# Holding each four gathers until the last four have landed, in a two-layer graph transformer on one core

## The chip, the cores and the metric

The kernel runs on one core of a Trainium2 chip. The metric is the time of one execution on the device, in microseconds, as a median over runs; lower is better. The engines are TensorE (PE in the rows, its weight loads PEld), VectorE (DVE), ScalarE (ACT), GpSimd (POOL) and SyncE (SP). Each has its own instruction queue, and they meet only through semaphores.

## The reference, cut to what matters

A graph has 3,125 nodes with 256 features and 50,000 edges sorted by destination. Two layers follow each other. Each adds a graph attention, a linear attention over all nodes and a mixture of experts to the node features.

```python
h = (x @ W.T).reshape(n, H, D)                       # layer 0: 8 heads of 32
alpha = einsum(h[src], a_src) + einsum(h[dst], a_dst) + sum(relu(edge_attr @ edge_W.T + b) * h[dst])
attn = segment_softmax(leaky_relu(alpha), dst)
out = segment_sum(h[src] * attn, dst)
...
# layer 1: two such convolutions in a row, 4 heads of 128, then 1 head of 256, without edge features
```

What matters here is `h[src]`: for every edge, the row of its source node is fetched from a table in HBM.

## The kernel before, in words

The edges lie in 196 blocks of 256, and the work goes over 220 windows (a block, cut where the destination tile of 128 nodes changes). The program is a list of stages. Each stage is a block in which all five engines run their own instruction lists; the next stage begins when all have ended.

A gather is one `indirect_dma_start` on GpSimd: 128 rows of a node table in HBM, chosen by an index column, are fetched into SBUF. GpSimd computes the descriptors, then the DMA engines move the rows. The gathers increment a semaphore of the buffer that they fill (`K.gath[q]`), and whoever uses the rows waits for it.

- `linear_attention_l0`: TensorE, ScalarE and VectorE compute the linear attention of layer 0 (25 tiles, five chunks of five). Beside it, GpSimd gathers the table rows (1,088 B) of the first 30 pairs of blocks, 4 gathers for each pair (line 793, three buffers, `GS` = 4). SyncE waits for each pair and stores it to HBM in edge order (lines 779 and 781); the gather of pair g waits for the store of pair g-3.
- `edge_scores_l0`: for 110 groups of two windows, VectorE makes one-hot matrices, TensorE multiplies (lines 1050 and 1054), ScalarE evacuates (1064), VectorE multiplies and sums (1110 and 1115). Beside it, GpSimd gathers the other 68 pairs, 4 gathers each (line 1033, six buffers). ScalarE copies the score terms out of each pair (line 1072, `sources`), in its own order between the evacuations, and SyncE stores the pair (1006). The gather of pair n waits for the copy and the store of pair n-6. ScalarE stands at the copy of pair n until its rows have landed, at a place in its list that is spread evenly over the 110 groups (`due`).
- `gather_rows` (line 1160) sets rows aside for every window of `STAGED` (66 of the 220, for each of the two convolutions of layer 1): 2 gathers for each window, five buffers, and a store to HBM for each window (`store_rows`, line 1170). It is called in five stages: `linear_attention_l1` (16 windows), the scores of the first convolution (40), its softmax (10), the scores of the second convolution (58) and its softmax (8). Rows have 2,064 B in the first convolution and 1,028 B in the second.
- `aggregate` (line 1603) gathers the remaining 154 windows of each convolution directly, 2 gathers a window, and is not touched.

Of the kernel before, what the change touches and what calls it, by code (L numbers as in the profile page):

```python
# [37 lines left out]
SUB = EB // P  # L38
# [674 lines left out]
def linear_attention_l0(prog, K, A):  # L713


    with Stage(prog, "mix0") as st:
        GS, QR = 2 * SUB, 3
# [35 lines left out]
        s_gath, gathered = K.gath, list(K.gathered)  # L753
# [9 lines left out]
        @block.sync  # L763
        def _(sp):
            sp.dma_start(wkv[:, :, 0:D], A["m0_wkt"].rearrange("(k p) n -> p k n", p=P)).then_inc(s_wkv, 16)
            sp.dma_start(wkv[:, :, D:2 * D], A["m0_wvt"].rearrange("(k p) n -> p k n", p=P)).then_inc(s_wkv, 16)
            load_rows(sp, s_w, gain[:, 0, :], A["m0_kg"])
            load_rows(sp, s_w, gain[:, 1, :], A["m0_vg"])
            load_rows(sp, s_w, shift[:, 0, :], A["m0_kb"])
            load_rows(sp, s_w, shift[:, 1, :], A["m0_vb"])  # L770
            sp.dma_start(wot[:, :, :], A["m0_wot"].rearrange("(k p) n -> p k n", p=P)).then_inc(s_w, 16)
            sp.dma_start(wq[:, :, :], A["m0_wq"].rearrange("(k p) n -> p k n", p=P)).then_inc(s_w, 16)
            sp.dma_start(enc_w[:, :], A["g0_enc"]).then_inc(s_encw, 16)
            load_rows(sp, s_bias, bias[:, 0, :], A["g0_b"])
            load_rows(sp, s_bias, bias[:, 1, :], A["m0_bo"])
            for g in range(EARLY0):
                q = g % QR
                sp.wait_ge(s_gath[q], gathered[q] + 16 * GS * (g // QR + 1))
                sp.dma_start(K.edge_h0[g * GS * P:(g + 1) * GS * P, :].rearrange("(k p) r -> p k r", p=P),
                             rows[:, q, :, 0:ROW0]).then_inc(s_kept[q], 16)  # L780
                sp.dma_start(home_of[g], rows[:, q, :, ROW0:ROW0 + H0]).then_inc(s_kept[q], 16)
            for q in range(QR):
                sp.wait_ge(s_kept[q], 32 * len(range(q, EARLY0, QR)))

        @block.gpsimd
        def _(pool):
            st.clear_stale(pool)
            for g in range(EARLY0):
                q = g % QR
                if g >= QR:  # L790
                    pool.wait_ge(s_kept[q], 32 * (g // QR))
                for k in range(GS):
                    pool.indirect_dma_start(rows[:, q, k, :], None, K.table0[:, :],  # L793
                                            bass.IndirectOffsetOnAxis(ap=K.src_blk[:, g * GS + k:g * GS + k + 1], axis=0)).then_inc(s_gath[q], 16)
# [147 lines left out]
def edge_scores_l0(prog, K, A):  # L942
# [6 lines left out]
    with Stage(prog, "score0") as st:  # L949
        G, Q, U2, QR = 2, 5, 2, 6  # L950
        GS = G * SUB
# [15 lines left out]
        s_gath, gathered = K.gath, list(K.gathered)  # L967
# [23 lines left out]
        @block.sync  # L991
        def _(sp):
            def load(g):
                q = g % Q
                if g >= Q:
                    sp.wait_ge(s_hot, g - Q + 1)
                    sp.wait_ge(s_en, G * (g - Q + 1))
                planes = K.edge_rows[g:g + 1, :].rearrange("g (m a e) -> g m a e", m=G, a=2)[:, :, 0, :]
                sp.dma_start(rel[:, q, :].rearrange("p (m e) -> p m e", m=G),
                             planes.partition_broadcast(P).rearrange("p g m e -> p (g m) e")).then_inc(s_load[q], 16)  # L1000
                sp.dma_start(attr[:, q, :], bass.AP(tensor=K.attr_parts.tensor, offset=g * (G * EB), ap=[[0, 3], [W * EB, R // 3], [1, G * EB]])).then_inc(s_load[q], 16)

            def keep(n):
                g, q = EARLY0 + n, n % QR
                sp.wait_ge(s_gath[q], gathered[q] + 16 * GS * (n // QR + 1))
                sp.dma_start(K.edge_h0[g * GS * P:(g + 1) * GS * P, :].rearrange("(k p) r -> p k r", p=P),
                             rows[:, q, :, 0:ROW0]).then_inc(s_kept[q], 16)

            for g in range(Q):
                load(g)  # L1010
            for g in range(groups):
                for n in range(due(g), due(g + 1)):
                    keep(n)
                if g + Q < groups:
                    load(g + Q)
            for n in range(due(groups), late):
                keep(n)
            sp.wait_ge(s_spread, W)
            sp.dma_start(pen, bass.AP(tensor=K.pen.tensor, offset=0, ap=[[L, C], [0, H], [1, L + 1]])).then_inc(s_pen, 16)
            for q in range(QR):  # L1020
                sp.wait_ge(s_kept[q], 16 * len(range(q, late, QR)))
            sp.wait_ge(s_pen, 16)

        @block.gpsimd
        def _(pool):
            st.clear_stale(pool)
            for n in range(late):
                g, q = EARLY0 + n, n % QR
                if n >= QR:
                    pool.wait_ge(s_copied, len(homes) + n - QR + 1)  # L1030
                    pool.wait_ge(s_kept[q], 16 * (n // QR))
                for k in range(GS):
                    pool.indirect_dma_start(rows[:, q, k, :], None, K.table0[:, :],  # L1033
                                            bass.IndirectOffsetOnAxis(ap=K.src_blk[:, g * GS + k:g * GS + k + 1], axis=0)).then_inc(s_gath[q], 16)
# [117 lines left out]
def gather_rows(pool, K, table, rows, windows, s_free):  # L1152

    Q = rows.shape[1]
    for n, w in enumerate(windows):
        q = n % Q
        if n >= Q:
            pool.wait_ge(s_free[q], 16 * (n // Q))
        for s in range(SUB):
            pool.indirect_dma_start(rows[:, q, s, :], None, table,  # L1160
                                    bass.IndirectOffsetOnAxis(ap=K.src_col[:, w * SUB + s:w * SUB + s + 1], axis=0)).then_inc(K.gath[q], 16)
# [19 lines left out]
def edge_scores_l1(prog, K, name, H, C, RW, table, kept, A):  # L1181
# [4 lines left out]
    with Stage(prog, name) as st:  # L1186
# [61 lines left out]
        @block.gpsimd  # L1248
        def _(pool):
            st.clear_stale(pool)  # L1250
            gather_rows(pool, K, table, held, STAGED[first:early], s_free)
# [115 lines left out]
def segment_softmax(prog, K, name, H, C, keep_max=None, RW=0, table=None, kept=None, A=None):  # L1367
# [8 lines left out]
    with Stage(prog, name) as st:  # L1376
# [43 lines left out]
        @block.gpsimd  # L1420
        def _(pool):
            st.clear_stale(pool)
            if blanks:
                pool.memset(zeros[:, :], 0.0).then_inc(s_zeros, 1)
            if late:
                gather_rows(pool, K, table, held, STAGED[early:], s_free)
# [822 lines left out]
def linear_attention_l1(prog, K, A):  # L2249

    KD = LH * LD
    with Stage(prog, "mix1") as st:
# [32 lines left out]
        @block.gpsimd  # L2285
        def _(pool):
            st.clear_stale(pool)
            gather_rows(pool, K, K.table1, held, STAGED[0:FIRST[H1]], s_free)
# [717 lines left out]
```

## Time and profile before

| | us |
|---|---|
| median of three runs | 3081.26 |
| range of the runs | 3078.65 to 3088.63 |
| span of the profiled execution | 3595.1 |

The profiled execution has no other time than its span: from its first instruction to its last 3595.1 us, 513.8 us more than the median of the runs. The rows below are from that one execution, with times in us from its first instruction. Busy means that an engine executes; idle time in brackets stands ahead of an instruction, with what ended it ("issue" and "remote" mean that the profile shows nothing that ended it just then). Ends of TensorE's matmuls are modelled.

### The profile page before, as it was taken

The numbers are of one execution on the slowest core, as the hardware profiler recorded it, in microseconds if no ns is written. First come the engines' busy times: TensorE is split into PE (matmuls) and PEld (weight loads), VectorE is DVE, ScalarE is ACT, GpSimd is POOL, SyncE is SP. The second block draws the span as 40 slices with busy tenths as digits, with TensorE's granted clock in tenths as the row PEclk, the third lists the DMA queues.
The fourth block names the chain that finished last, engine by engine and source line by source line (L and its number), as shares of the span: only waits on it lengthen the run. The fifth ranks groups of instructions, "written<-read, shape, count | busy, mean of one in ns | idle before, by whom it ended". The sixth has DMA issues, their size and how long they took to land. (4 is left out here: it accounts for less than half of the span.)

```text
span 3595.1 us, 47970 instructions
## 1 busy us (share of the span) xinstructions
PE 2251.7 (63%) x11012; PEld 1557.3 (43%) x11013; DVE 2033.2 (57%) x4073; ACT 1091.0 (30%) x3339; POOL 1519.1 (42%) x1534
## 2 busy tenths in 40 slices
PE   3333567677578738976666498897703556666543
PEld 3112233333456535553455377675602434444432
DVE  6328455556788844325268577677504645555733
ACT  3103232333300122215200465664400055556311
POOL 1660544453000020112453777775472166666044
PEclk9755566655799959998867799998855677777577
DMA  4870555565287628862697787786686344444066
GB/s 140 227 203 0 157 176 178 166 184 170 93 237 230 195 86 258 268 221 92 242 392 255 231 249 245 242 245 203 186 220 172 85 126 128 127 130 130 7 203 192
DMA packets 450407, 655.70 MB, mean 182 GB/s; under 512 B 68320, under 2 KB 329310, under 8 KB 449683
## 3 DMA queue, kind: packets, MB, share of 16 engines
q1 hardware_dynamic: 330003, 351.74, 31.7%
q0 software_dynamic: 84944, 255.17, 24.1%
q10 hardware_dynamic: 35296, 46.90, 3.7%
q8 instruction: 66, 1.08, 0.1%
q14 instruction: 98, 0.80, 0.1%
HBM read 485.21 MB, written 169.74 MB: 182 GB/s over the span
## 5 line engine op out<-in xcount | busy, mean ns | idle before, releaser
L1603 POOL DMA_INDIRECT xn<-table,src_col x572 | 617.5, 1080 | 246.1 <-issue 155.7
L1646 PE MATMUL sum_h_ps<-xn,sum_h_hot 128*128 128x261 f32 (+1 forms) x1936 | 556.4, 439 | 226.3 <-DVE xn L1660 103.2
L1646 PEld LDWEIGHTS sum_h_ps<-xn,sum_h_hot 128*128 128x128 f32 x1936 | 404.2, 217 | 369.5 <-issue 169.9
L1160 POOL DMA_INDIRECT arena_a<-table,src_col x264 | 268.0, 1015 | 388.9 <-issue 321.1
L1669 DVE TENSOR_TENSOR arena_a<-arena_a,sum_h_ps 128x522 f32 (+1 forms) x440 | 246.4, 560 | 305.2 <-issue 115.4
L1033 POOL DMA_INDIRECT arena_b<-table,al x272 | 257.5, 947 | 360.1 <-ACT arena_a L1072 185.5
L1054 PE MATMUL score_ps_hd<-arena_a,score_hot 128*128 x1320 | 289.4, 382 | 0.0
L1110 DVE TENSOR_TENSOR xn<-xn,score_ps_hd 128x528 f32<-128x528 f32 x220 | 154.4, 702 | 228.1 <-remote 144.5
L1660 DVE TENSOR_TENSOR xn<-xn,al 128x514 f32<-128x514 f32 (+1 forms) x352 | 242.9, 690 | 45.8 <-issue 19.4
L1754 PE MATMUL sum_ps<-xn,sum_hot 128*128 128x264 f32 x880 | 210.6, 393 | 52.2 <-DVE sum_hot L1764 34.2
L1050 PE MATMUL score_ps_en<-enc_rows,score_attr 30*128 30x256 bf16 x440 | 119.4, 367 | 186.5 <-DVE xn L1110 122.5
L1064 ACT ACTIVATE xn<-score_ps_en 128x512 f32<-128x512 f32 x220 | 129.9, 595 | 343.0 <-PE score_ps_en L1050 204.4
L1754 PEld LDWEIGHTS sum_ps<-xn,sum_hot 128*128 128x128 f32 x880 | 162.4, 190 | 100.4 <-issue 75.5
L1054 PEld LDWEIGHTS score_ps_hd<-arena_a,score_hot 128*128 128x128 bf16 x1320 | 146.7, 125 | 125.2 <-issue 78.0
L1646 PE MATMUL sum_h_ps<-arena_b,sum_h_hot 128*128 128x261 f32 x704 | 177.1, 400 | 31.2 <-DVE arena_b L1660 26.2
L1768 DVE TENSOR_TENSOR xn<-xn,al 128x528 f32<-128x528 f32 x220 | 154.6, 703 | 32.1 <-DMA xn<-edge_h 30.7
L1615 ACT ACTIVATE sum_h_hot<-sum_h_away,sum_h_one 128x256 f32<-128x256 f32 x220 | 111.7, 508 | 191.0 <-DMA score_attr<-attr_parts 78.9
L1631 ACT ACTIVATE xn<-xn,al 128x129 f32<-128x129 f32 x528 | 167.3, 388 | 0.0
L1646 PEld LDWEIGHTS sum_h_ps<-arena_b,sum_h_hot 128*128 128x128 f32 x704 | 137.9, 198 | 61.6 <-DVE arena_b L1660 29.8
L793 POOL DMA_INDIRECT xn<-table,al x120 | 117.0, 975 | 91.2 <-issue 91.2
L1115 DVE TENSOR_REDUCE al<-xn 128x16 f32<-128x528 f32 x220 | 152.9, 695 | 0.0
L1610 ACT ACTIVATE sum_h_away<-iota_row,rel_col 128x128 f32<-128x128 f32 x440 | 149.1, 386 | 0.0
(531 smaller groups left out, 4127.5 us busy)
## 6 DMA issues: line engine op xcount, KB each, us to landing
xn<-edge_h SPq DMA_DIRECT2D x220, 264.0 KB, 3.0
edge_h<-arena_b SPq DMA_DIRECT2D x68, 528.0 KB
arena_b<-kept SPq DMA_DIRECT2D x66, 516.0 KB
xn_t<-edge_rows SPq DMA_DIRECT2D x110, 256.0 KB, 4.7
score_h_hot<-hots SPq DMA_DIRECT2D x220, 128.0 KB
kept<-arena_a ACTq DMA_DIRECT2D x40, 516.0 KB
xn<-kept SPq DMA_DIRECT2D x66, 257.0 KB
arena_a<-in_f_w SPq DMA_DIRECT2D x16, 1024.0 KB, 8.6
```

Of the source, the lines that this page charges most:

```text
L1033: pool.indirect_dma_start(rows[:, q, k, :], None, K.table0[:, :], bass.IndirectOffsetOnAxis(ap=K.src_blk[:, g * GS + k:g * GS + k + 1], ax ...
L1054: ins = pe.matmul(ps_hd[:, m, s, 0:D + H], lhsT=hot[:, q, edges[s]], rhs=near[:, window, c, :], start=(c == 0), stop=(c == 2))
L1110: dve.tensor_tensor(prod[:, w % U3, :].rearrange("p (s d) -> p s d", s=SUB), enc[:, m, :].rearrange("p (s d) -> p s d", s=SUB), ps_hd[:, m ...
L1115: dve.tensor_reduce(al[:, w * SUB:(w + 1) * SUB, :], prod[:, w % U3, :].rearrange("p (s h r) -> p s h r", s=SUB, h=H), AX, ALU.add).then_i ...
L1160: pool.indirect_dma_start(rows[:, q, s, :], None, table, bass.IndirectOffsetOnAxis(ap=K.src_col[:, w * SUB + s:w * SUB + s + 1], axis=0)). ...
L1603: pool.indirect_dma_start(rows[w][:, s, 0:RW], None, table, bass.IndirectOffsetOnAxis(ap=K.src_col[:, w * SUB + s:w * SUB + s + 1], axis=0 ...
L1631: ins = act.activation(cols, cols, ACT.Copy, scale=al[:, w * SUB + 1, h:h + 1])
L1646: ins = pe.matmul(ps[:, u, b, 0:part], lhsT=hot[:, w % QH, s, :], rhs=rows[w][:, s, b * part:(b + 1) * part], start=(s == 0), stop=(s == S ...
L1660: dve.tensor_tensor(view, view, al[:, bass.ds(w * SUB, HALF), :].rearrange("p s h -> p (s h)").unsqueeze(2).broadcast_to([P, HALF * H, RW ...
L1669: dve.tensor_tensor(out, out, ps[:, j % U2, :, 0:part], ALU.add).then_inc(s_acc, 1)
L1754: ins = pe.matmul(ps[:, bass.ds(banks[j % 4], 1), 0:ROW0].rearrange("p a c -> p (a c)"), lhsT=hot[:, q, s, :], rhs=rows[:, q, s, :], start ...
L1768: dve.tensor_tensor(view, view, al[:, bass.ds(w * SUB, SUB), :].unsqueeze(3).broadcast_to([P, SUB, H, R]), ALU.mult).then_inc(s_msg, 1)
```

## The change

In each of the three places where such gathers are issued, GpSimd waits, before it issues the next four, until the semaphore shows that the last four have landed. The waits that were there (for a free buffer) stay. No gather, buffer or store is added or moved.

```diff
                 if g >= QR:
                     pool.wait_ge(s_kept[q], 32 * (g // QR))
+                if g:
+                    pool.wait_ge(s_gath[(g - 1) % QR], gathered[(g - 1) % QR] + 16 * GS * ((g - 1) // QR + 1))
                 for k in range(GS):
...
                     pool.wait_ge(s_kept[q], 16 * (n // QR))
+                if n:
+                    pool.wait_ge(s_gath[(n - 1) % QR], gathered[(n - 1) % QR] + 16 * GS * ((n - 1) // QR + 1))
                 for k in range(GS):
...
         if n >= Q:
             pool.wait_ge(s_free[q], 16 * (n // Q))
+        if n and n % 2 == 0:
+            pool.wait_ge(K.gath[(n - 1) % Q], K.gathered[(n - 1) % Q] + 16 * SUB * ((n - 1) // Q + 1))
         for s in range(SUB):
```

## Rows read from the trace of the kernel before

**Rows 1.** The page's first line.
```profile
span 3595.1 us, 47970 instructions
```
**Rows 2.** Windows: stretch, length, PE, PEld, DVE, ACT, POOL busy (instructions), PEclk, DMA, GB/s.
```profile
104.00:360.00 256.00, 93.59 (x212) 44.43 (x212) 123.88 (x158) 45.77 (x50) 117.03 (x120) 0.62 0.48 137
360.00:927.00 567.00, 384.44 (x1760) 173.38 (x1760) 324.82 (x582) 167.90 (x511) 257.54 (x272) 0.62 0.56 165
984.00:1253.00 269.00, 216.07 (x896) 166.53 (x896) 229.48 (x661) 16.40 (x42) 0.00 (x0) 0.99 0.75 221
...
2010.00:2502.00 492.00, 416.81 (x1760) 341.61 (x1760) 362.37 (x661) 299.24 (x1101) 356.51 (x318) 0.94 0.78 237
...
2579.00:2847.00 268.00, 91.19 (x983) 70.36 (x983) 108.83 (x268) 0.00 (x0) 109.84 (x116) 0.54 0.62 176
...
2875.00:3337.00 462.00, 299.19 (x880) 200.50 (x880) 234.60 (x442) 264.49 (x881) 311.35 (x308) 0.75 0.46 126
```
**Rows 3.** Windows of 10 us in the scores of the second convolution.
```profile
2710.00:2720.00 10.00, 0.56 (x3) 0.42 (x4) 0.00 (x0) 0.00 (x0) 7.58 (x8) 0.50 0.83 211
...
2750.00:2760.00 10.00, 6.56 (x106) 5.32 (x105) 10.00 (x27) 0.00 (x0) 0.00 (x0) 0.50 0.63 188
```
**Rows 4.** Timeline of TensorE, layer-0 linear attention: start, length, merged count, [idle before].
```profile
108.06 18.91 PE L803 MATMUL mix_ps_kv<-mix_wkv,xn_t 128*128 128x512 f32 x40 [18.19 <-DMA mix_wkv<-in_m_wvt]
```
**Rows 5.** Timeline of ScalarE in the same stage.
```profile
155.93 0.60 ACT L830 ACTIVATE arena_a<-mix_ps_kv 128x512 f32<-128x512 f32 x1 [10.71 <-remote]
...
276.12 1.57 ACT L830 ACTIVATE arena_a<-mix_ps_kv 128x512 f32<-128x512 f32 x3 [0.53 <-remote]
```
**Rows 6.** Timeline of GpSimd in the same stage: first and last gather of one pair.
```profile
131.61 0.95 POOL L793 DMA_INDIRECT xn<-table,al  x1 [0.30 <-issue]
...
135.37 0.94 POOL L793 DMA_INDIRECT xn<-table,al  x1 [0.30 <-issue]
```
**Rows 7.** Timeline of SyncE in the same stage: the store of that pair.
```profile
138.32 0.37 SPq L779 DMA_DIRECT2D edge_h<-xn  x1
```
**Rows 8.** Timeline of VectorE in the same stage.
```profile
119.12 2.82 DVE L871 TENSOR_REDUCE mix_gsum<-arena_a 128x40 f32<-128x2560 f32 x1 [2.39 <-issue]
...
284.87 2.81 DVE L871 TENSOR_REDUCE mix_gsum<-arena_a 128x40 f32<-128x2560 f32 x1
...
306.37 2.81 DVE L871 TENSOR_REDUCE mix_gsum<-arena_a 128x40 f32<-128x2560 f32 x1
...
359.05 0.98 DVE L934 SCALAR_TENSOR_TENSOR enc_rows<-mix_enc_parts,mix_part_is,enc_rows 30x256 bf16<-30x256 bf16 x2
```
**Rows 9.** Timeline of VectorE at the end of the layer-0 scores.
```profile
886.96 0.70 DVE L1110 TENSOR_TENSOR xn<-xn,score_ps_hd 128x528 f32<-128x528 f32 x1 [0.39 <-PE score_ps_hd L1054]
...
890.89 0.70 DVE L1110 TENSOR_TENSOR xn<-xn,score_ps_hd 128x528 f32<-128x528 f32 x1 [0.39 <-PE score_ps_hd L1054]
...
897.08 0.70 DVE L1110 TENSOR_TENSOR xn<-xn,score_ps_hd 128x528 f32<-128x528 f32 x1
...
899.80 0.70 DVE L1110 TENSOR_TENSOR xn<-xn,score_ps_hd 128x528 f32<-128x528 f32 x1
```
**Rows 10.** By source line, the gathers: ns min/median/max, first and last start.
```profile
L793 POOL DMA_INDIRECT xn<-table,al x120: 942/947/1689, 105.5 to 257.8; - x120
L1033 POOL DMA_INDIRECT arena_b<-table,al x272: 941/947/1068, 361.4 to 875.5; - x136
```
**Rows 11.** Timelines of GpSimd and SyncE, first softmax of layer 1: last gather, last store.
```profile
2001.46 0.95 POOL L1160 DMA_INDIRECT arena_a<-table,src_col  x1 [0.30 <-issue]
...
2007.51 0.36 SPq L1170 DMA_DIRECT2D kept<-arena_a  x1
```
**Rows 12.** Timelines of GpSimd and ScalarE's queue, second scores: last gather, last six stores.
```profile
2728.95 0.95 POOL L1160 DMA_INDIRECT arena_a<-table,src_col  x1 [0.30 <-issue]
...
2720.03 12.79 ACTq L1170 DMA_DIRECT2D kept<-arena_a  x6
```
**Rows 13.** Waits of GpSimd: total, times, longest.
```profile
POOL arena_a L1160 <- DMA kept<-arena_a: 42.1, 27, 3.9
```

## The prediction

> **What bounds the kernel now.** I read the page first, against the times of the runs. The profiled execution lasts 3595.1 us [rows 1], the median run 3081.26: the profile holds 513.8 us, a sixth of the runs' time, that the runs do not have. Before any wait is costed it must be known where they lie, because a gate on GpSimd is free beside a stalled engine and dear beside a busy one.
>
> The stretches by stage [rows 2] show it. In the layer-0 sum, a stage without gathers, VectorE is busy 229 of 269 us. In the layer-0 scores it is busy 325 of 567, in the layer-0 linear attention 124 of 256, in the second scores 109 of 268: every stage in which GpSimd gathers has long holes. The windows of 10 us name the cause inside one stage [rows 3]. While GpSimd issues 8 gathers in 10 us, TensorE starts 3 matmuls and VectorE nothing; after the last gather the same stage runs 106 matmuls and a VectorE that is never idle. The timelines show what it is that comes late [rows 4, 5]. TensorE is through its first 40 matmuls (ten tiles, four each) at 126.97, but ScalarE evacuates the tenth tile only at 155.93, with 10.71 us of idle time that nothing in the profile ended. After the last gathers, three tiles follow within 1.57 us. So the completions of finished matmuls are held up while GpSimd gathers, and come in a bunch when it stops. The gathers are not held up: the last of a pair ends at 135.37 + 0.94 = 136.31 and SyncE starts the store that waits for it at 138.32, 2.0 us later [rows 6, 7].
>
> Do the runs have these stalls? Without them each stage takes the longer of two lines, GpSimd's and that of the other engines. GpSimd needs 1.25 us a gather (131.61 to 135.37 is three steps), 5.0 us for four.
> - Layer-0 linear attention: 120 gathers end at 257.8 + 0.95 [rows 10]; 2.0 for landing and as much, an estimate, for the last store give about 263. The other engines: VectorE's first chunk starts at 119.12, an undisturbed chunk takes 306.37 - 284.87 = 21.5, and from the last chunk's start to the end are 360.0 - 306.4 = 53.7 [rows 8]: 119.1 + 4 x 21.5 + 53.7 = 259. So 263 instead of 360: 97 us less.
> - Layer-0 scores: 68 x 5.0 = 340. The other engines take 2.72 us a group where VectorE ends last (899.80 - 897.08) and 3.93 where it waits for TensorE (890.89 - 886.96) [rows 9], for 110 groups 299 or 432. The profile takes 519 from the first gather to the landing of the last (361.4 to 875.5, and four gathers and 2.0 on top) [rows 10]. So 340 to 432: 87 to 179 less.
> - Second scores: 58 windows of two gathers are 145; VectorE's work in the stage is 109 [rows 2]. With some 5 for landing and store, 150 instead of 268: 118 less.
> - The two sums over edges: 154 windows x 2 x 1.25 = 385 for GpSimd, 492 and 462 in the profile [rows 2]: up to 184 less.
>
> Together that is 302 to 578 us less, and 513.8 are missing in the runs. They fit without the stalls, and best where GpSimd sets the pace. No other idle time in these rows comes near to 514 us. I therefore take it that the stalls belong to the profiled execution, and that in the runs GpSimd's line is the longest, or level with it, in the gated stages. The Trainium skill, "NOTIFIC — the notification-queue block", section 7.1, says that the unit that writes trace records pushes back on its producers when it is full inside, so that a record path can throttle an engine. By that rule profiling would hold up completions and the runs would be free of it, as in my forecast; no row here shows records, and the sum does without it.
>
> **The change part by part.** It removes nothing and moves no instruction. It adds 157 gates: 29 in the layer-0 linear attention (30 pairs), 67 in the layer-0 scores (68 pairs), 28 in the second scores (58 windows), and 33 in the others (7, 19, 4 and 3). A gate lasts from the end of the fourth gather to its landing. Behind it on GpSimd stand only the next gathers; for those wait SyncE's or ScalarE's stores and, in the layer-0 scores, ScalarE's copies, with all evacuations behind them. The gate's own price is not in the trace; the nearest row is SyncE's wait for the same semaphore, 2.0 us after the fourth gather's end [rows 6, 7]. GpSimd already leaves 0.30 us between gathers, so a gate costs 1.7: four gathers take 6.7 us instead of 5.0. It can't cost nothing, since four rows' worth of transfer cannot have landed when their descriptors have just been written.
> - Layer-0 linear attention: 29 x 1.7 = 49. GpSimd's line goes from 263 to 312; the others end at 259 and cover none of it. In the profiled execution the same 49 would lie under the stalls (312 is short of 360).
> - Layer-0 scores: 68 x 6.7 = 456. From 340 that is 116, from 432 it is 24. The six buffers do not help, since it is the rate that falls, not a delay: ScalarE's copies are spread evenly over the groups, so each late pair holds up the evacuations. The missing 513.8 asks for the fast pace, and TensorE got a share of 0.99 of its clock in the layer-0 sum [rows 2]; I take 105.
> - Second scores: the last store starts at 2732.45 (the six end at 2732.82, 0.37 each), 2.55 after the last gather's end at 2729.90 [rows 12]. So a gate is 1.7 to 2.25, 28 gates 48 to 63, and the 40 us between 109 and 150 cover none of it, as GpSimd is the longer line. I take 56.
> - The other 33 gates, where rows are twice as wide in all but three: 1.7 to 4.8 each. The upper end is the softmax, where the last store starts 5.1 us after the last gather's end (2002.41 to 2007.51) [rows 11], with stores and earlier gathers in its way; a gate thins that traffic out. That is 56 to 158, less up to 42 that GpSimd waits for stores there now [rows 13] and that the gates absorb: 14 to 116. I take 45, nearer to the low end, since the first scores also have TensorE and VectorE work beside the gathers.
>
> The sum is 49 + 105 + 56 + 45 = 255 us. Against the profile's own time it can't be added up: most of it would vanish under stalls in the 3595.1 us, and only the softmax stages, where stores end last, would show it. It is added to the median, which is 513.8 below that span: 3081 + 255 = 3336. The ends: 45 + 24 + 40 + 14 = 123 and 55 + 125 + 63 + 116 = 359, if landing varies by some tenths of a us: 3204 to 3440. The Trainium skill, "DMA: Bandwidth & Descriptors", "Anatomy of one DMA", gives about 2.0 us of fixed cost a transfer, mostly the receipt of its end, and its "Rules for kernel authors" say to issue early and wait late so that this overlaps. Rows 6 and 7 agree with the 2.0 us; by that rule alone 157 gates would be 314 us, an estimate, and 3395.
>
> **The rivals.**
> - *The stalls are real, and thinner gathers relieve them (faster).* In the runs, too, completions would wait for gathers. Then a pair of 6.7 us has a quarter of its time free of gathers, and the three large stages lose a quarter of their excess of 97, 179 and 118: 394 / 4 = 99 less. The seven softmax gates give back 12 to 34, say 20: about 3002. It decides if more than some 250 of the 513.8 us are something else than stalls. For it: rows 3 to 5 tie the stalls to gathers tightly. Against it: no other place for 514 us.
> - *Only the softmax stages pay.* If the other engines in the runs need as long as GpSimd's new line (312 rather than 259 in the linear attention, 456 in the scores), the gates are hidden there and 7 x 1.7 to 4.8 = 12 to 34 remain: 3093 to 3115, say 3098. For it: the slow pace of 3.93 comes near in the scores. Against it: 259 and 109 are far below.
> - *The gates do not bind*, and nothing changes: 3081. A gate asks for the count of the four gathers just issued, which land 2.0 us later, so it must bind.
>
> **How the numbers follow.** The forecast has 0.83, the real stalls 0.09, the softmax alone 0.07, no effect 0.01. A measurement of this kernel can tell about 0.3% (9 us) from no change. Faster takes the first rival, 0.09. Same takes the last and a third of the softmax case, 0.03. Slower is the rest, 0.88. The predicted time is 3336. The range of 3215 to 3415 leaves out the ends beyond which several terms must err together, and all the rivals, some 0.2.
>
> **What would show it.** In the changed profile the first of four gathers stands behind 1.7 to 2.3 us of idle time at lines 793 and 1033. The gathers of line 793 end near 308 and not 259, and 272 gathers of line 1033 take at least 456 us. The span of the profile rises by less than the runs do, or falls, because thinner gathers stall TensorE less there: its excess over the runs shrinks below 400 us. I am wrong on the cause if the runs get faster or stay, and on a size if one stage hides its gates: the scores above all, if VectorE's groups follow at 3.93 us.

## The result and the profile after

The kernel takes 3480.28 us with the change (median of four runs, 3478.43 to 3487.75) against 3082.23 before (median of four runs, one more than in the table above): a ratio of 1.1297, with a 95% interval of 1.128 to 1.1313, or 398 us more. The prediction was 3336, the end of its range 3415. The direction came out as forecast, and so did the way a gate costs (GpSimd stands idle until the rows have landed); the size is 398 instead of 255 us.

The page of the changed kernel: its first line [rows 1], the gathers of the layer-0 scores, and VectorE's one-hot matrices there (busy time, mean ns of one, then the idle time ahead and what ended most of it).

```profile
span 3479.8 us, 48048 instructions
...
L1037 POOL DMA_INDIRECT arena_b<-table,al x272 | 257.1, 945 | 264.7 <-DMA arena_b<-table,al 119.9
...
L1107 DVE TENSOR_SCALAR score_hot<-score_rel,iota_part 128x512 bf16<-128x512 bf16 x110 | 38.9, 353 | 189.8 <-DMA score_attr<-attr_parts 189.8
```

The profiled execution took 3481.43 us for a span of 3479.8: this profile has none of the 513.8 us that the profile of before had over its runs. The gathers at 1037 now stand behind 264.7 us of idle time, more than they take.

The windows by stage [rows 2]: layer-0 linear attention, layer-0 scores, `linear_attention_l1`, first scores, first softmax, second scores, second softmax; and two windows of 10 us in the second scores [rows 3].

```profile
103.90:338.40 234.50, 70.71 (x212) 40.20 (x212) 124.25 (x158) 45.02 (x51) 120.83 (x120) 0.63 0.52 149
338.40:882.20 543.80, 363.45 (x1760) 167.45 (x1760) 321.13 (x581) 167.82 (x511) 257.09 (x272) 0.68 0.61 172
1674.70:1746.80 72.10, 41.33 (x209) 29.53 (x209) 10.52 (x24) 18.12 (x53) 30.23 (x32) 0.74 0.77 242
1746.80:1950.10 203.30, 93.63 (x1772) 83.31 (x1772) 133.35 (x247) 0.00 (x0) 80.17 (x80) 0.78 0.89 290
1950.10:2008.10 58.00, 13.15 (x48) 6.80 (x48) 25.42 (x20) 10.76 (x23) 30.14 (x20) 0.53 0.59 182
...
2520.90:2777.50 256.60, 82.02 (x983) 67.15 (x983) 108.11 (x268) 0.00 (x0) 109.98 (x116) 0.54 0.64 184
2777.50:2814.80 37.30, 4.39 (x18) 2.60 (x18) 10.32 (x20) 4.09 (x6) 16.54 (x16) 0.50 0.42 113
```
```profile
2560.00:2570.00 10.00, 6.54 (x106) 5.36 (x104) 10.00 (x27) 0.00 (x0) 3.78 (x4) 0.50 0.99 297
...
2680.00:2690.00 10.00, 0.00 (x0) 0.00 (x0) 0.00 (x0) 0.00 (x0) 3.78 (x4) 0.50 0.53 143
```

In the second scores VectorE is busy for all of the first window, while GpSimd gathers: no completion is held up. In the second window nothing runs but four gathers in 10 us. GpSimd's line alone is what the stage waits for there.

How one gate looks, in the timelines of GpSimd and SyncE in the layer-0 linear attention [rows 6, 7]: the first and the last gather of one pair and the first of the next, and then the store that waits for the same four rows.

```profile
130.72 0.94 POOL L795 DMA_INDIRECT xn<-table,al  x1 [2.56 <-DMA xn<-table,al]
...
134.68 0.95 POOL L795 DMA_INDIRECT xn<-table,al  x1 [0.30 <-issue]
138.21 1.15 POOL L795 DMA_INDIRECT xn<-table,al  x1 [2.59 <-DMA xn<-table,al]
```
```profile
137.49 0.38 SPq L779 DMA_DIRECT2D edge_h<-xn  x1
```

The fourth gather ends at 135.63. SyncE sees the landing and starts its store 1.86 us later, near the 2.0 of the prediction. GpSimd, which waits for the same semaphore, starts its next gather 0.72 us after that.

By source line [rows 10], and VectorE's last instruction of the stage [rows 8]:

```profile
L795 POOL DMA_INDIRECT xn<-table,al x120: 940/946/1870, 104.9 to 331.8; - x120
...
L1037 POOL DMA_INDIRECT arena_b<-table,al x272: 940/946/979, 339.2 to 853.7; - x136
```
```profile
261.23 0.98 DVE L936 SCALAR_TENSOR_TENSOR enc_rows<-mix_enc_parts,mix_part_is,enc_rows 30x256 bf16<-30x256 bf16 x2
```

VectorE is done at 262, the gathers at 332.8: 70 us of gathers with nothing beside them but their own stores. GpSimd's waits [rows 13] (total, times, longest):

```profile
POOL arena_a L1166 <- DMA arena_a<-table,src_col: 256.3, 60, 6.7
...
POOL arena_b L1037 <- DMA arena_b<-table,al: 119.9, 40, 4.1
...
POOL xn L795 <- DMA xn<-table,al: 77.8, 29, 6.2
POOL arena_b L1037 <- ACT arena_a L1076: 73.1, 27, 3.0
```

The mean wait is 77.8 / 29 = 2.7 us at 795, (119.9 + 73.1) / 67 = 2.9 at 1037 (ScalarE's copy, named in 27 of them, reads the rows of the same four gathers, and most likely ends just before GpSimd restarts without being what GpSimd waits for), and 256.3 / 60 = 4.3 at 1166. The prediction had 2.0, and took off 0.30 that is there without a gate.

### The profile page after: what moved, and what is told of

Its sections match the earlier page's. It is cut to its first block and busy times, and to the rows that moved or that the text cites. A ratio compares the mean times of both kernels' runs of the same rounds, so it can differ in the third digit from the quotient of the medians.

```text
span 3479.8 us, 48048 instructions
## 1 busy us (share of the span) xinstructions
PE 2145.8 (62%) x11012; PEld 1492.5 (43%) x11013; DVE 2037.1 (59%) x4073; ACT 1100.7 (32%) x3339; POOL 1490.3 (43%) x1534
## 5 line engine op out<-in xcount | busy, mean ns | idle before, releaser
L1609 POOL DMA_INDIRECT xn<-table,src_col x572 | 588.0, 1028 | 181.1 <-issue 154.7
L1652 PE MATMUL sum_h_ps<-xn,sum_h_hot 128*128 128x261 f32 (+1 forms) x1936 | 532.4, 419 | 199.1 <-DVE xn L1666 150.8
L1652 PEld LDWEIGHTS sum_h_ps<-xn,sum_h_hot 128*128 128x128 f32 x1936 | 375.0, 204 | 348.7 <-DVE xn L1666 248.5
L1166 POOL DMA_INDIRECT arena_a<-table,src_col x264 | 267.1, 1012 | 430.0 <-DMA arena_a<-table,src_col 256.3
L1037 POOL DMA_INDIRECT arena_b<-table,al x272 | 257.1, 945 | 264.7 <-DMA arena_b<-table,al 119.9
L1058 PE MATMUL score_ps_hd<-arena_a,score_hot 128*128 x1320 | 273.2, 365 | 0.0
L1058 PEld LDWEIGHTS score_ps_hd<-arena_a,score_hot 128*128 128x128 bf16 x1320 | 141.2, 121 | 114.9 <-issue 73.1
L1054 PEld LDWEIGHTS score_ps_en<-enc_rows,score_attr 30*128 30x128 bf16 x440 | 26.2, 100 | 342.5 <-DVE xn L1114 192.1
L1652 PE MATMUL sum_h_ps<-arena_b,sum_h_hot 128*128 128x261 f32 x704 | 166.5, 383 | 0.9 <-DVE arena_b L1666 0.6
L1107 DVE TENSOR_SCALAR score_hot<-score_rel,iota_part 128x512 bf16<-128x512 bf16 x110 | 38.9, 353 | 189.8 <-DMA score_attr<-attr_parts 189.8
```

The lines of the kernel that those rows point to most:

```text
L1058: ins = pe.matmul(ps_hd[:, m, s, 0:D + H], lhsT=hot[:, q, edges[s]], rhs=near[:, window, c, :], start=(c == 0), stop=(c == 2))
L1166: pool.indirect_dma_start(rows[:, q, s, :], None, table, bass.IndirectOffsetOnAxis(ap=K.src_col[:, w * SUB + s:w * SUB + s + 1], axis=0)). ...
L1609: pool.indirect_dma_start(rows[w][:, s, 0:RW], None, table, bass.IndirectOffsetOnAxis(ap=K.src_col[:, w * SUB + s:w * SUB + s + 1], axis=0 ...
L1652: ins = pe.matmul(ps[:, u, b, 0:part], lhsT=hot[:, w % QH, s, :], rhs=rows[w][:, s, b * part:(b + 1) * part], start=(s == 0), stop=(s == S ...
```

## The experiments

Times of experiments are medians against the kernel before on the same chip, with the 95% interval of the ratio. An edit is shown against the kernel before.

**Each of the three places alone.** Three kernels, each with one of the three hunks of the diff: the one at line 793, the one at 1033, the one in `gather_rows`.

> The 29 gates of the layer-0 linear attention alone. As predicted (1.7 us a gate, the landing as SyncE sees it less the usual 0.30 between gathers): 49 us slower than before. If a gate costs what the changed kernel's trace shows ahead of a gated gather (2.57 us idle, 2.27 more than usual, and 6.2 at the first): 70 us slower. If the stage's other engines end later in the runs than I reckoned (259), less than 35 us. If the stalls of the profiled execution are in the runs too: within 10 us of before, or faster.

> The 67 gates of the layer-0 scores alone. As predicted: 105 us slower than before (116 if all gates bind, 24 if the other engines go at 3.93 us a group). By the idle time in the changed kernel's trace (2.81 us, 2.5 more than usual): 67 x 2.5 = 168 us if GpSimd sets the pace of the stage in the runs of before, 76 if the pace there is 3.93 us a group (432 us, and GpSimd's line now 508). If the stalls are real: within 10 us of before, or faster.

> The 61 gates in the stages of layer 1 that set rows aside, alone. As predicted: 56 + 45 = 101 us slower. By the idle time in the changed kernel's trace (285.6 us ahead of 65 gathers, 266 more than usual), less the 42 us that GpSimd waits for stores before: 224 us, and what the other engines of the first scores cover less again; if it is more than 170, the price of a gate here, 3.5 to 6 us beside stores and loads, is what the prediction missed most. If the stalls are real: faster or within 10 us of before.

| gates | us more than before | ratio | predicted | a gate |
|---|---|---|---|---|
| 29, layer-0 linear attention | 63 | 1.0211 (1.0177 to 1.0244) | 49 | 2.2 |
| 67, layer-0 scores | 164 | 1.0537 (1.0509 to 1.0566) | 105 | 2.5 |
| 61, layer 1 | 157 | 1.0515 (1.0490 to 1.0540) | 101 | 2.6 |

Together they are 384 of the 398 us: three separate costs, and no relief from one to another. In each place a gate costs more than 1.7 us in the mean. That the runs have the stalls and thinner gathers relieve them is out, and so is a cost in the softmax stages alone. (In `gather_rows` the gate asks for the last two of the four gathers only, the second window's.)

**The gate one group later.**
```diff
+                if g > 1:
+                    pool.wait_ge(s_gath[(g - 2) % QR], gathered[(g - 2) % QR] + 16 * GS * ((g - 2) // QR + 1))
...
+                if n > 1:
+                    pool.wait_ge(s_gath[(n - 2) % QR], gathered[(n - 2) % QR] + 16 * GS * ((n - 2) // QR + 1))
...
+        if n > 3 and n % 2 == 0:
+            pool.wait_ge(K.gath[(n - 3) % Q], K.gathered[(n - 3) % Q] + 16 * SUB * ((n - 3) // Q + 1))
```

> All three gates, but each waits for the group of four before the last, so that four gathers more are under way. If a gate's price is the landing that GpSimd stands through, that landing (1.8 to 5.4 us behind the fourth gather) lies under the next four gathers (5.0 us) and nearly all of the 398 us is given back: within 0 to 25 us of before. If the price is the waiting instruction itself, or the semaphore's way to GpSimd, 0.4 to 0.7 us a gate stays: 60 to 110 us slower. If it is the thinned traffic, most of the 398 us stays.

5 us slower, 1.0020 (1.0006 to 1.0034). GpSimd's waits in this kernel:

```profile
POOL arena_a L1166 <- DMA kept<-arena_a: 56.6, 47, 4.4
POOL arena_a L1166 <- DMA arena_a<-table,src_col: 14.9, 17, 1.9
...
POOL arena_b L1037 <- DMA arena_b<-table,al: 8.4, 13, 1.4
POOL arena_b L1037 <- ACT arena_a L1076: 5.9, 9, 1.5
POOL xn L795 <- DMA xn<-table,al: 2.7, 7, 0.9
```

Nearly as many waiting instructions, and almost no waiting for landings (the waits for stores, `kept`, are there without gates too): what costs is the landing that GpSimd stands through, not the instruction. This is what the Trainium skill, "DMA: Bandwidth & Descriptors", "Rules for kernel authors", advises (issue early, wait late); by 393 of 398 us it holds here.

**The kernel before, profiled again**, without an edit.

> The kernel before, unchanged, with a new profile. If the late completions of TensorE came from gathers issued without a gate while a profile is taken, as the prediction holds, the span of this profile is again some 500 us above the time of the runs, and the layer-0 scores again take about 567 us of it. If they belonged to that one execution alone, the span is within 20 us of 3083, the layer-0 linear attention takes about 166 us, the layer-0 scores about 373 and the second scores about 167, as in the ungated stages of the kernels with a part of the gates.

The execution took 3077.63 us and its span is 3076.0. Its page's first line; the windows of the seven stages with gates; ScalarE's tenth tile of the linear attention [rows 5].

```profile
span 3076.0 us, 47970 instructions
```
```profile
104.00:270.40 166.40, 70.69 (x212) 40.08 (x212) 124.62 (x158) 45.01 (x51) 123.56 (x120) 0.69 0.74 210
270.40:644.70 374.30, 274.87 (x1760) 140.44 (x1760) 318.38 (x581) 166.30 (x511) 258.63 (x272) 0.91 0.85 250
1436.50:1490.60 54.10, 39.58 (x209) 28.58 (x209) 10.51 (x24) 18.11 (x53) 30.31 (x32) 0.86 0.93 323
1490.60:1658.50 167.90, 111.16 (x1772) 101.61 (x1772) 138.94 (x247) 0.00 (x0) 76.87 (x80) 0.72 0.95 351
1658.50:1705.60 47.10, 13.42 (x48) 6.89 (x48) 25.42 (x20) 10.75 (x23) 31.62 (x20) 0.50 0.72 225
...
2220.30:2385.00 164.70, 82.04 (x984) 66.82 (x984) 108.21 (x268) 0.00 (x0) 111.61 (x116) 0.57 0.93 286
2385.00:2413.20 28.20, 4.39 (x18) 2.56 (x18) 10.47 (x20) 4.08 (x6) 15.87 (x16) 0.50 0.56 150
```
```profile
126.32 0.60 ACT L830 ACTIVATE arena_a<-mix_ps_kv 128x512 f32<-128x512 f32 x1 [1.12 <-PE mix_ps_kv L803]
```

The tenth tile is evacuated at 126.32 and not at 155.93, at nearly the same pace of gathers. So gathers by themselves do not hold up TensorE's completions, profiled or not: the 513.8 us belonged to that one execution. The seven stages now compare one to one: +68.1, +169.5, +18.0, +35.4, +10.9, +91.9 and +9.1, together 403 us, all but 1 of the 403.8 between the two spans.

**What a gate's price hangs on in the linear attention.** The gate at 793, and one more in each pair:
```diff
                 for k in range(GS):
+                    if k == 2:
+                        pool.wait_ge(s_gath[q], gathered[q] + 16 * GS * (g // QR) + 32)
```

> The layer-0 linear attention alone, gated after each two gathers: 59 gates in place of 29. If a gate's price is a latency that hardly depends on what is under way (landing 1.83 us behind the last gather's end, 0.72 from there to the next gather, less the usual 0.30): 59 x 2.25 = 133 us slower than before, about twice the 63 us of 29 gates. If the landing is mostly the transfer of what is still under way, a gate on half the rows costs half: 60 to 75 us, as with 29 gates.

124 us slower, 1.0393 (1.0375 to 1.0410): twice 63, or 2.1 us a gate. GpSimd's wait is 2.4 us in the mean:

```profile
POOL xn L797 <- DMA xn<-table,al: 143.8, 59, 4.4
```

In this stage the price is a latency, and hardly depends on how many rows are still to land.

**Half of the gates**: against the changed kernel,
```diff
-                if g:
+                if g and g % 2 == 0:
...
-                if n:
+                if n and n % 2 == 0:
...
-        if n and n % 2 == 0:
+        if n and n % 4 == 0:
```

> Every second gate of all three places: 76 gates (14, 33 and 29) in place of 157, each after eight gathers. If every gate binds and has the price found alone (63/29, 165/67 and 157/61 us): 30 + 81 + 75 = 186 us slower than before. If the drained queue of eight gathers takes longer to land than that of four, more than 220; if half the gates hide under what the other engines have left, less than 150.

224 us slower, 1.0727 (1.0706 to 1.0749), 38 more than the 186 that half of the gates would cost at the prices found alone. By the stage windows the linear attention is at 35 us for 14 gates, 2.5 each, little above the 2.2 of before. The scores are at 132 us for 33, 4.0 each instead of 2.5, and GpSimd's waits there say the same:

```profile
POOL arena_b L1037 <- DMA arena_b<-table,al: 89.7, 20, 5.2
...
POOL arena_b L1037 <- ACT arena_a L1076: 51.4, 13, 4.7
```

These are 4.3 us a gate, 4.0 above the usual 0.30. Layer 1 is left with some 57, less than the 75 expected. So in the scores something else makes the landing late; the last two kernels below look for it.

**Why gates are dearer in layer 1.** The gates of layer 1, and stores by pairs of windows, in `store_rows`:
```diff
         queue.wait_ge(K.gath[q], K.gathered[q] + 16 * SUB * (n // Q + 1))
+        if n % 2 == 0 and n + 1 < count:
+            queue.wait_ge(K.gath[(n + 1) % Q], K.gathered[(n + 1) % Q] + 16 * SUB * ((n + 1) // Q + 1))
```

> The 61 gates of layer 1 as in the kernel that cost 157 us alone, but the store of the first window of each four gathers now waits for the second window's rows too, so that both stores run beside the next four gathers. If the dearer gates of layer 1 come from the first window's store, which starts at the fourth gather's start and shares the DMA engines with its rows: the idle time ahead of a gated gather in the quiet half of the second scores falls from 3.4 to about 2.6 us, and 30 to 60 of the 157 us come back (97 to 127 slower than before). If they come from the rows' own width or from the loads beside them: 150 to 165 slower, as without the edit.

142 us slower, 1.0457 (1.0439 to 1.0474): 15 came back, half of the least that the theory of the store had asked for. GpSimd's timeline in the quiet half of the second scores, first of the kernel with the gates alone, then with the edit: the fourth gather and the next one.

```profile
2444.88 0.94 POOL L1162 DMA_INDIRECT arena_a<-table,src_col  x1 [0.30 <-issue]
2449.16 0.95 POOL L1162 DMA_INDIRECT arena_a<-table,src_col  x1 [3.33 <-DMA arena_a<-table,src_col]
```
```profile
2415.84 0.95 POOL L1162 DMA_INDIRECT arena_a<-table,src_col  x1 [0.30 <-issue]
2419.31 0.94 POOL L1162 DMA_INDIRECT arena_a<-table,src_col  x1 [2.52 <-DMA arena_a<-table,src_col]
```

In the quiet half the store accounts for the whole difference: 2.5 us, as in the linear attention of layer 0. Some 18 gates by 0.8 us are 14 of the 15 us. Beside the loads of one-hot planes, in the first half and in the first scores, the waits stayed mostly between 4.2 and 7.4 us.

So loads were put into the quiet half, on top of that edit:
```diff
+            if H == 1:
+                sp.wait_ge(s_mm, QL + W // G)
+                for n in range(200):
+                    q, g = n % QL, n % (W // G)
+                    sp.wait_ge(s_load[q], 16 * (turns + n // QL))
+                    sp.dma_start(hot_bits[:, q, :], K.hots[g * P:(g + 1) * P, :]).then_inc(s_load[q], 16)
...
```

> The kernel with stores by pair and gates in layer 1 (142 us slower than before), and in the second scores 200 more loads of 128 KB, of one-hot planes that are no longer used, ten under way at a time, once the stage's matmuls are done: the loads of the stage's first half are so repeated beside the gathers of its quiet half, without any work of the other engines. If it is the loads that make a gate there cost 4 to 6 us of idle time instead of 2.6: idle times of 4 to 6 us come up again beside them, some 18 gates by 1.5 to 3 us, 27 to 55 us more: 169 to 197 slower than before. If it was the other engines' work, the idle times stay at 2.6 and the time at 135 to 150 slower.

178 us slower, 1.0567 (1.0550 to 1.0585), 36 more than without these loads. GpSimd's timeline and the window beside the loads:

```profile
2444.56 0.95 POOL L1162 DMA_INDIRECT arena_a<-table,src_col  x1 [0.30 <-issue]
2451.85 0.95 POOL L1162 DMA_INDIRECT arena_a<-table,src_col  x1 [6.34 <-DMA arena_a<-table,src_col]
```
```profile
2400.00:2500.00 100.00, 15.16 (x71) 12.94 (x69) 7.66 (x19) 0.00 (x0) 36.33 (x39) 0.59 1.07 320
```

With the DMA engines full (share 1.07) and the other engines nearly idle, the wait is as long as in the first half of the stage in the kernel without these loads (4.2 to 6.6). The Trainium skill, "DMA: Bandwidth & Descriptors", "Rules for kernel authors", says that transfers issued by different engines run on the same 16 DMA engines and interleave; this run agrees, 6.3 us beside the loads against 2.5 without them.

**How far ahead a wait must look.** The same gates, ahead of the third gather of the next four (in `gather_rows`, of every second window):
```diff
                 for k in range(GS):
+                    if g and k == 2:
+                        pool.wait_ge(s_gath[(g - 1) % QR], gathered[(g - 1) % QR] + 16 * GS * ((g - 1) // QR + 1))
...
+                    if n and k == 2:
+                        pool.wait_ge(s_gath[(n - 1) % QR], gathered[(n - 1) % QR] + 16 * GS * ((n - 1) // QR + 1))
...
+        if n > 2 and n % 2:
+            pool.wait_ge(K.gath[(n - 2) % Q], K.gathered[(n - 2) % Q] + 16 * SUB * ((n - 2) // Q + 1))
```

> All three gates, but each stands ahead of the third gather of the next four instead of the first: two gathers, 2.5 us, are issued while the last four land. If a gate's price is the landing that nothing covers: nothing in layer 0, where the landing takes 1.8 to 2.1 us, and in layer 1 what is left of 3.4 to 5.9 us, 0.6 to 3 us a gate, less what GpSimd waits for stores there anyway: 20 to 70 us slower than before in all. If what counts is how few gathers are under way (six here, four in the change, eight with the gate a group later): about half of the 398 us, 150 to 230.

122 us slower, 1.0399 (1.0378 to 1.0420), which neither theory had. By its stage windows the linear attention is 3 us longer than ungated, as the landing says, but the layer-0 scores are 80 us longer, where none were expected; layer 1 has the other 39. With the gate of the change the landing there took 2.9 - 0.72 = 2.2 us, which two gathers would have covered. Now 2.5 us of gathers and 1.5 of waiting, less 0.72, make it 3.3. Two kernels asked whether the stage's own loads (128 KB of window rows and 30 KB of edge attributes a group) are the reason. They leave out most of these loads, so that the matmuls of that stage work on data of earlier groups; the second one has no gates:
```diff
+                few = P if g < Q else 1
...
+                             planes.partition_broadcast(few).rearrange("p g m e -> p (g m) e")).then_inc(s_load[q], 16)
+                copies = 3 if g < Q else 1
...
```

> The kernel with the gates two gathers later (122 us slower, 80 of them in the layer-0 scores), but in the layer-0 scores the loads beside the gathers are cut to a sliver from the sixth group of windows on: one partition instead of 128 of the window rows and 10 rows instead of 30 of the edge attributes, so that the matmuls there work on data of earlier groups. If the landing in this stage is late because of the loads that share the DMA engines: the idle time ahead of the gated gather falls from 1.5 to 0.3 us as in the linear attention, and the kernel is 35 to 60 us slower than before. If it is the pair's own store or the gathers themselves: 110 to 125, as with the loads.

> The control: the kernel before, without gates, with the same loads cut to a sliver in the layer-0 scores. GpSimd's line, 272 gathers by 1.25 us, sets the pace there and doesn't depend on the loads: within 10 us of before. If the loads themselves cost more than that, the time of this kernel is the one to compare the other with.

With the later gates 40 us slower, 1.0139 (1.0119 to 1.0158); without gates 6 us faster, 0.9979 (0.9969 to 0.9990). GpSimd's waits in the scores with the loads and the later gates, and with the later gates alone (the line is 1039 there):

```profile
POOL arena_b L1037 <- DMA arena_b<-table,al: 103.1, 67, 2.5
```
```profile
POOL arena_b L1039 <- issue: 85.8, 261, 6.6
```

The window of the layer-0 scores: loads and later gates, later gates alone, neither.

```profile
273.90:727.40 453.50, 335.83 (x1760) 159.20 (x1760) 321.14 (x581) 168.80 (x511) 258.42 (x272) 0.75 0.72 206
```
```profile
273.60:644.40 370.80, 274.03 (x1760) 140.60 (x1760) 316.86 (x581) 166.45 (x511) 258.08 (x272) 0.91 0.72 210
```
```profile
269.50:638.40 368.90, 275.73 (x1760) 141.12 (x1760) 318.32 (x581) 166.90 (x511) 257.98 (x272) 0.91 0.72 211
```

103.1 / 67 = 1.5 us a gate with the loads, and next to nothing but the usual 0.30 without them. Without the loads the later gates cost 2 us in this stage instead of 80, and 47 in the whole kernel instead of 122: what remains lies in layer 1, but for some 3 or 4 us. The rate at which the DMA engines move bytes is not the reason, as it is no lower without the loads (210 GB/s against 206). Why these loads hold up the rows more than the gathers' own traffic does is open.

## Why the prediction was right in direction and wrong in size

**That the runs lack the 513.8 us, and GpSimd's line is the longest.** Right for the three large terms. The new profile of before has stages of 166.4, 374.3 and 164.7 us where the prediction had 263 - 104 = 159, then 340 to 432, then 150. In the layer-0 scores the 272 gathers took 341 us of the 374, at 1.25 us each: the fast end was the true one. (The 519 us that the prediction set beside this should be 517, since 875.5 is the start of the last single gather; nothing hangs on it.) It is wrong for the first scores, where VectorE, and not GpSimd, ended last. The last gather of that stage and VectorE's last instruction, first in the new profile of before (stage of 1490.6 to 1658.5), then in the changed kernel (1746.8 to 1950.1):

```profile
1627.95 0.95 POOL L1160 DMA_INDIRECT arena_a<-table,src_col  x1 [0.30 <-issue]
```
```profile
1655.17 2.84 DVE L1347 SCALAR_TENSOR_TENSOR xn<-al 128x128 f32<-128x128 f32 x14
```
```profile
1941.94 0.95 POOL L1166 DMA_INDIRECT arena_a<-table,src_col  x1 [0.30 <-issue]
```
```profile
1883.04 2.85 DVE L1353 SCALAR_TENSOR_TENSOR xn<-al 128x128 f32<-128x128 f32 x14
```

Before, VectorE ended 29 us behind the gathers; with the gates the gathers end 57 us behind VectorE. The gathers ended 58 us later in the stage, the stage became 35 longer: 22 us of its gates are covered.

**Why they lack them.** Wrong. The prediction tied the stalls to gathers in a profiled execution. The second profile of the same kernel has the same gathers and no stalls, and no other profile here has them either. What happened in that one execution, and why its late completions fell together with the gathers, is open. The rule that the prediction named (the Trainium skill, "NOTIFIC — the notification-queue block", section 7.1) is shown at work by no run here. The conclusion did not need this cause: the times of the runs carried it.

**The step that failed: "a gate costs 1.7: four gathers take 6.7 us instead of 5.0".** The term was mis-sized in two ways.
- The nearest row was SyncE's wait, and GpSimd restarts 0.72 us after SyncE. In the linear attention four gathers take 138.21 - 130.72 = 7.5 us, the idle time ahead of a gate is 2.59 and its price 2.29. That is 0.59 more than 1.7, for 157 gates 93 of the missed 143 us, worked out.
- The landing was taken from a stage with little beside the gathers. In the layer-0 scores the wait is 2.9 us; that the loads there make the landing late is shown for the later gate (1.5 us of waiting), and only likely for the change's own. In layer 1 it is 4.3; in the second scores, where it was tried, that is for the first window's store (3.33 - 2.52 = 0.8 us) and the loads (6.34 - 2.52, up to 3.8). That the rows of the first convolution, twice as wide, add to it was not tried by itself.

**The terms.** Linear attention 49, measured 63; the gathers end at 332.8 and not near 308, and VectorE ends at 262, so nothing covers them, as said. Layer-0 scores 105, measured 164; 11 us had been kept back for a slower pace of the other engines, and every gate binds. Second scores 56, in the stage windows 92; the 40 us between VectorE's work and GpSimd's line covered none of it, as said. The other 33 gates 45, in the windows 73: their wait was put near the low end of 1.7 to 4.8, and is near the high one (4.2 above the usual gap, in the mean of 32). That a wait of 4.3 us in layer 1 made the stages only 165 us longer for 61 gates has two reasons. The gates absorb the waits for stores that GpSimd had there before, as the prediction said, 67.4 us in the new profile:

```profile
POOL arena_a L1160 <- DMA kept<-arena_a: 67.4, 53, 4.7
```

And the first scores cover 22 us. With the usual 0.30 taken off each wait, 238 - 52 - 22 = 164. The missed 143 us are spread over all four, as a price that is too low does.

**The rivals.** There are no stalls in the runs for thinner gathers to relieve, and each of the seven stages became longer. One relief is there all the same: in the first scores VectorE was done 139 us after the start of the stage instead of 167, with the DMA engines less full (0.89 against 0.95). What sped VectorE up was not tried by itself. The gates are hidden nowhere but for the 22 us there; and they bind.

**What the prediction asked the profile to show.** Idle time of 1.7 to 2.3 us at the gates of 793 and 1033: about 2.6 and 2.9, too low again. At least 456 us for the gathers of 1033: 854.6 - 339.2 = 515. An excess of the span below 400 us: it is 0, but in the new profile of before too, so that this says nothing of thinner gathers.

## What to carry to other kernels

A wait for the transfers just issued costs their whole landing each time wherever the waiting engine sets the pace of the stage, and the price is the idle time on the engine that waits: restart included, and in the stage where it stands, since other transfers on the same engines made it 2.5 to 6.3 us here. The same wait, one group of four further back, cost 5 us in place of 398; in layer 0, two gathers further back was far enough where nothing was loaded beside them. And when a profile's span does not agree with the times of the runs, take a second profile before explaining the first.

## What the runs showed of the hardware

GpSimd restarts late after a wait for VectorE too, not only after a landing. In the experts of layer 0, VectorE's result is there at 1396.39 + 0.42 = 1396.81, and GpSimd, which waits for it, starts 0.66 us later (timelines of VectorE and GpSimd in the changed kernel):

```profile
1396.39 0.42 DVE L2059 TENSOR_TENSOR al<-moe_ps_y,moe_b 128x256 f32<-128x256 f32 x1 [3.03 <-PE moe_ps_y L2032]
```
```profile
1397.47 0.55 POOL L2083 DMA_DIRECT2D y_slots<-al  x1 [2.89 <-DVE al L2059]
```

TensorE's granted clock was lower with the gates: in the layer-0 scores a mean of 0.91 of full speed without them and 0.68 with them, between its two levels of 1.0 (2.4 GHz) and 0.5 (1.2 GHz), and the same 1760 matmuls took 363 us of its time instead of 275. TensorE waited longer for work in that stage: VectorE's one-hot matrices stood 189.8 us behind loads (21.4 in the new profile of before), which queue on SyncE behind the stores that wait for landings. The slower TensorE did not hold up GpSimd: all idle time ahead of the gathers at 1037 is that of the 67 gates (119.9 + 73.1) or of the 205 other gathers (71.7, so 0.35 each), and the stage ended 28 us after its last gather, not later than without gates (32).
